# Inner rows of a quantised feed-forward block: turned by DMA in place of TensorE, for tiles 1 to 7

## The chip, the cores and the metric

The kernel runs on one core of one Trainium2 chip. The metric is the device time of one execution in microseconds (us). Each time is the median of several runs. The profile is of one execution of its own.

## What is computed

Two decoder blocks work on x (1024 rows of 512 numbers) and a context of the same size. Each block is an attention over the context and a feed-forward part, both added to x behind a gate. The feed-forward part of the first block is quantised to integers, rows to 8 bits and weights to 4:

```python
def _fake_quant_act(x, n_bits=8):
    scale = max(|x| over the row) / 127
    return clip(round(x / scale), -128, 127) * scale
...
gate = _quant_linear(x, Wg)          # 512 -> 1376
up = _quant_linear(x, Wu)            # 512 -> 1376
h = silu(gate) * up                  # the inner row, 1376 numbers
return _quant_linear(h, Wd)          # 1376 -> 512, the down product
```

The second block is an attention with softmax (queries and keys from the context, values from x) and a small routed low-rank layer on top of a dense one:

```python
R = q @ k ; attention = softmax(R) ; out = attention @ v
y = x @ W_base.T + b_base + sum over experts of alpha * (x @ A.T) @ B.T
```

## The kernel before

x is cut into 8 tiles of 128 rows. A first program (0 to about 555 us) does the whole first attention and prepares the quantised weights. Behind it stands a second program, `last_programs`, which takes the 8 tiles through the quantised feed-forward, the second attention and the routed layer. Several tiles are in flight at once. The order of the work is written out by hand, one list of calls for each of the five engines, and each call waits on semaphores, so an engine never passes a call whose input is late. SyncE (SP) has such a list for its DMAs too.

One tile t goes this way (the names are those of the calls):

- `gate_mm(t, n)`, `up_mm(t, n)` on TensorE for the three column groups n of 512, 512 and 352; `scale_gate`, `scale_up` on VectorE; `tanh_half` on ScalarE; `product` on GpSimd; `make_h(t, n)` on VectorE. The row h is complete after n = 2.
- `h_scales(t)` on VectorE takes the row's largest number; `h_shifted(t)` on ScalarE (L2754) scales h and adds a magic number, so that the low 16 bits of each float are a 2-byte float near 1536 that holds the integer.
- `h_transpose_a(t)` (8 blocks, L1739) and `h_transpose_b(t)` (3 blocks, L1746) on TensorE turn these low halves by a product with an identity, into PSUM banks 4 and 5, which are also those of `gate_mm` and `up_mm`.
- `hT_copy_a(t)` (L2759, 1024 columns) and `hT_copy_b(t)` (L2764, L2765) on ScalarE take off 1536 and write the integers as bf16 into `hqT`.
- `down(t)` (L1754) on TensorE, 11 matmuls of `hqT` with `W.T_d` into bank 4; `output(t)` on VectorE (L2307, tile `f_y`), `add(t)` on GpSimd, and then the statistics, `normalise(t)` and `v_item(t)` of the second attention.

The second attention of tile t has 8 pieces n: `logits(t, n)` on TensorE (L1778, L1779) into bank 0 or 6, `row_max` on VectorE (L2334), `exps` on ScalarE (L2798, tile `b_e`), `reciprocal` for two pieces at a time on VectorE (L2339), `weigh` on GpSimd (L3146), `weights_T` on TensorE (L1788) into bank 3, `copy_T` on ScalarE (L2807, tile `b_eT`), and `attend_pair`. Three limits set how far TensorE may go ahead: `logits` number m waits until `exps` number m-2 has read the bank; `weights_T` number m waits for `weigh` m and for `copy_T` m-1, since bank 3 is one; and `row_max` stands in VectorE's list in a fixed place beside `output`.

SP issues `load_ctx` (context of later tiles), `duplicate` (L1638, five DMAs that lay out queries and keys) and `store`.

Of the kernel before, what the change touches and what calls it, by code (L numbers as in the profile page):

```python
# [7 lines left out]
ACT = mybir.ActivationFunctionType  # L8
# [6 lines left out]
P = 128  # L15
B, S, D = 16, 64, 512
NT = B * S // P
DC = D // P
# [1493 lines left out]
def late_buffers(cx, K):  # L1512
# [75 lines left out]
    M.low_w = take("l1_low", [P, DC, P + E_ACT])  # L1588
    M.bT = M.e[0]
# [51 lines left out]
def last_programs(cx, K, M, W, W1, L0, ctx_dram, out_dram):  # L1641
# [3 lines left out]
    if True:  # L1645
# [27 lines left out]
        s_hTa, s_hTa_sb = sem("s_f_hTa"), sem("s_f_hTa_sb")  # L1673
        s_hTb, s_hTb_sb = sem("s_f_hTb"), sem("s_f_hTb_sb")
# [34 lines left out]
        def tensor(pe, first):  # L1709
# [26 lines left out]
            def h_transpose_a(t):  # L1736
                pe.wait_ge(s_hq, t + 1)
                for c in range(8):
                    mm = pe.transpose(hT_a[:, c, :], low_half(h[t % 2])[:, c * P:(c + 1) * P], K.ident_b[:, :])  # L1739
                mm.then_inc(s_hTa, 1)  # L1740

            def h_transpose_b(t):
                pe.wait_ge(s_hq, t + 1)
                for c in range(8, FT):
                    w = P if c < FT - 1 else FL
                    mm = pe.transpose(hT_b[0:w, c - 8, :], low_half(h[t % 2])[:, c * P:c * P + w], K.ident_b[:, :])  # L1746
                mm.then_inc(s_hTb, 1)

            def down(t):
                pe.wait_ge(s_hTa_sb, t + 1)  # L1750
                pe.wait_ge(s_hTb_sb, t + 1)
# [57 lines left out]
            def x3_T(t):  # L1809
# [3 lines left out]
                if t == NT - 1:  # L1813
                    pe.wait_ge(s_hTb_sb, NT)
# [98 lines left out]
            h_transpose_b(0)  # L1913
            pe.wait_ge(s_gate, 6)
            h_transpose_a(0)
            pe.wait_ge(s_qk_lo[1], 3)
            qk(2, 0)
            pe.wait_ge(s_hTb_sb, 1)
            up_mm(1, 2)
            weights_T(0, 5)  # L1920
            pe.wait_ge(s_hTa_sb, 1)
# [25 lines left out]
            pe.wait_ge(s_gate, 8)  # L1947
            h_transpose_a(1)
            logits(1, 6)
            pe.wait_ge(s_up, 8)  # L1950
            h_transpose_b(1)
# [3 lines left out]
            pe.wait_ge(s_hTa_sb, 2)  # L1955
            gate_mm(2, 2)
            logits(1, 7)
            pe.wait_ge(s_hTb_sb, 2)
# [26 lines left out]
            pe.wait_ge(s_up, 10)  # L1985
            h_transpose_b(2)
# [5 lines left out]
            pe.wait_ge(s_gate, 11)  # L1992
            h_transpose_a(2)
            logits(2, 5)
            pe.wait_ge(s_hTb_sb, 3)
            up_mm(3, 1)
            weights_T(2, 1)
            pe.wait_ge(s_hTa_sb, 3)
            down(2)
            logits(2, 6)  # L2000
            weights_T(2, 2)
            logits(2, 7)
            pe.wait_ge(s_out, 3)
            gate_mm(3, 2)
            weights_T(2, 3)
            pe.wait_ge(s_up, 11)
            up_mm(3, 2)
# [18 lines left out]
            pe.wait_ge(s_gate, 12)  # L2026
            h_transpose_a(3)
            pe.wait_ge(s_up, 12)
            h_transpose_b(3)
# [6 lines left out]
            pe.wait_ge(s_hTa_sb, 4)  # L2036
# [1456 lines left out]
```

## Time and profile before

| | us |
|---|---|
| median of 3 runs (770.85 to 773.05) | 772.27 |
| the profiled execution | 772.25 |
| its span, first to last instruction | 770.4 |
| PE (TensorE) busy | 747.7, 97% |
| DVE (VectorE) busy | 593.2, 77% |
| ACT (ScalarE) busy | 489.8, 64% |
| POOL (GpSimd) busy | 500.3, 65% |

Busy shares are of the whole span. PE's are modelled from the starts of its instructions, so that a short wait can hide in them. The time of an execution is 1.85 us more than its span.

### The profile page before, as it was taken

The numbers are of one execution on the slowest core, as the hardware profiler recorded it, in microseconds if no ns is written. First come the engines' busy times: TensorE is split into PE (matmuls) and PEld (weight loads), VectorE is DVE, ScalarE is ACT, GpSimd is POOL, SyncE is SP. The second block draws the span as 40 slices with busy tenths as digits, with TensorE's granted clock in tenths as the row PEclk, the third lists the DMA queues.
The fourth block names the chain that finished last, engine by engine and source line by source line (L and its number), as shares of the span: only waits on it lengthen the run. The fifth ranks groups of instructions, "written<-read, shape, count | busy, mean of one in ns | idle before, by whom it ended". The sixth has DMA issues, their size and how long they took to land.

```text
span 770.4 us, 13672 instructions
## 1 busy us (share of the span) xinstructions
PE 747.7 (97%) x4829; PEld 594.3 (77%) x4829; DVE 593.2 (77%) x1138; ACT 489.8 (64%) x1082; POOL 500.3 (65%) x431
## 2 busy tenths in 40 slices
PE   8998899999999999999999999997999999999997
PEld 7876688888888888888878888775656777787776
DVE  5888888867788776677866666777899997898863
ACT  5756666665567545665555555354589898888772
POOL 2678676656657865567884557645377877787762
PEclk9999999999999999999999999998999999999999
DMA  9310454433453133241224201265254333122101
GB/s 339 115 68 28 130 113 98 119 83 102 115 133 91 51 99 93 71 130 52 69 57 107 68 1 44 27 257 163 68 152 104 90 91 89 39 64 59 49 18 40
DMA packets 74640, 71.03 MB, mean 92 GB/s; under 512 B 48412, under 2 KB 49660, under 8 KB 74188
## 3 DMA queue, kind: packets, MB, share of 16 engines
q1 hardware_dynamic: 74284, 69.82, 32.2%
q8 instruction: 39, 0.64, 0.3%
q10 hardware_dynamic: 288, 0.33, 0.2%
q14 instruction: 29, 0.24, 0.1%
HBM read 49.04 MB, written 6.34 MB: 72 GB/s over the span
## 4 chain that ended last, share of the span: by engine, by line
PE 83%; DVE 7%; ACT 4%; POOL 3%; issue 1%; DMA 1%; SPq 0%; DVEq 0%
PE bank L81 11%; PE bank L83 10%; PE bank L82 10%; PE bank L591 7%; PE bank L596 6%; PE bank L592 6%; PE bank L1802 4%; PE bank L573 4%; PE bank L675 4%; PE bank L1788 3%; PE bank L1754 2%; PE bank L1725 2%; PE bank L1733 2%; PE bank L1778 2%; PE bank L1779 2%
## 5 line engine op out<-in xcount | busy, mean ns | idle before, releaser
L1346 POOL TENSOR_TENSOR rope_swap<-rope_swap,trig 128x512 f32<-128x512 f32 x80 | 105.2, 1315 | 135.0 <-ACT rope_swap L761 134.7
L1055 DVE SCALAR_TENSOR_TENSOR x_res<-bank,gate,x_res 128x512 f32<-128x512 f32 x128 | 95.5, 746 | 54.1 <-PE bank L596 53.8
L888 ACT CAST oT_hi<-bank 128x512 fp32r<-128x512 f32 x64 | 34.4, 590 | 126.3 <-PE bank L675 126.3
L591 PE MATMUL bank<-wo_hi,oT_hi 128*128 128x512 f32 x256 | 102.4, 400 | 7.2 <-DVE x_res L1055 6.7
L81 PE MATMUL bank<-xnT_hi,wq_hi 128*128 128x512 f32 x252 | 101.5, 403 | 0.0
L592 PE MATMUL bank<-wo_lo,oT_hi 128*128 128x512 f32 x256 | 101.4, 396 | 0.0
L83 PE MATMUL bank<-xnT_hi,wq_lo 128*128 128x512 f32 x252 | 100.0, 397 | 0.0
L82 PE MATMUL bank<-xnT_lo,wq_hi 128*128 128x512 f32 x252 | 99.5, 395 | 0.0
L1352 POOL TENSOR_TENSOR q_rope<-rope_cos,rope_swap 128x512 f32<-128x512 f32 x64 | 82.9, 1295 | 5.0
L596 PE MATMUL bank<-wo_hi,oT_lo 128*128 128x512 f32 x256 | 80.7, 397 | 4.3 <-DVE oT_lo L1211 4.3
L3146 POOL TENSOR_TENSOR b_e<-b_e,b_inv 128x512 f32<-128x512 f32 x64 | 68.3, 1081 | 18.9 <-DVE b_inv L2339 18.4
L1012 DVE TENSOR_TENSOR rope_cos<-bank,trig 128x512 f32<-128x512 f32 x80 | 53.9, 674 | 30.1 <-PE bank L83 26.2
L768 ACT COPY row_other<-row_max 32x16 f32<-32x16 f32 x256 | 51.6, 202 | 23.8 <-DVE row_max L1026 15.5
L760 ACT COPY rope_swap<-bank 64x512 f32<-64x512 f32 x80 | 46.7, 584 | 29.1 <-DVE rope_cos L1012 26.0
L591 PEld LDWEIGHTS bank<-wo_hi,oT_hi 128*128 128x128 f32 x256 | 48.9, 191 | 20.1 <-DVE x_res L1055 9.1
L596 PEld LDWEIGHTS bank<-wo_hi,oT_lo 128*128 128x128 f32 x256 | 48.8, 191 | 15.6 <-DVE oT_lo L1211 5.2
L81 PEld LDWEIGHTS bank<-xnT_hi,wq_hi 128*128 128x128 f32 x252 | 47.3, 188 | 13.0 <-issue 0.3
L592 PEld LDWEIGHTS bank<-wo_lo,oT_hi 128*128 128x128 f32 x256 | 48.9, 191 | 10.5
L1359 POOL TENSOR_TENSOR prob<-prob,row_inv 128x512 f32<-128x512 f32 x32 | 33.6, 1049 | 35.1 <-DVE row_inv L1046 35.1
L83 PEld LDWEIGHTS bank<-xnT_hi,wq_lo 128*128 128x128 f32 x252 | 47.3, 188 | 11.1
L82 PEld LDWEIGHTS bank<-xnT_lo,wq_hi 128*128 128x128 f32 x252 | 47.3, 188 | 10.7
L761 ACT COPY rope_swap<-bank 64x512 f32<-64x512 f32 x80 | 46.3, 578 | 0.9
(277 smaller groups left out, 1955.4 us busy)
## 6 DMA issues: line engine op xcount, KB each, us to landing
wq_raw<-in_wq_tiles SPq DMA_DIRECT2D x16, 512.0 KB, 3.7
wo_raw<-in_L_xattn_wo SPq DMA_DIRECT2D x16, 512.0 KB, 4.1
xn<-in_L_ffn_Wd SPq DMA_DIRECT2D x16, 256.0 KB, 2.9
b_ctx<-in_ctx SPq DMA_DIRECT2D x32, 128.0 KB, 2.6
b_k_twice<-b_qk_hi SPq DMA_DIRECT2D x32, 128.0 KB, 2.4
w_T_dram<-w_out SPq DMA_DIRECT2D x28, 128.0 KB, 3.0
w_T<-w_T_dram SPq DMA_DIRECT2D x2, 1376.0 KB, 9.6
xn<-in_L_ffn_Wg SPq DMA_DIRECT2D x10, 256.0 KB, 3.9
```

What stands on the lines that cost most here:

```text
L81: pe.matmul(out, a_hi, b_hi, start=first, stop=False)
L82: pe.matmul(out, a_hi, b_lo, start=False, stop=False)
L83: return pe.matmul(out, a_lo, b_hi, start=False, stop=last)
L591: pe.matmul(out, oT_hi[:, tl, h], wo_hi[jp][:, h, :], start=(h == 0), stop=False)
L592: pe.matmul(out, oT_hi[:, tl, h], wo_lo[jp][:, h, :], start=False, stop=False)
L596: mm = pe.matmul(out, oT_lo[:, tl, h], wo_hi[jp][:, h, :], start=False, stop=(h == 1))
L768: act.copy(row_other[other, U % 2, :], row_max[mine, U % 2, :]).then_inc(s_swap, 1)
L1012: dve.tensor_tensor(out=rope_cos[:, rp, :].rearrange("p (b s) -> p b s", s=S), in0=proj[stream % NPROJ][:, :].rearrange("p (b s) -> p b s" ...
L1055: dve.scalar_tensor_tensor(out=K.x[:, t, :], in0=wo_ps[t % 2][:, :], scalar=K.gate[:, 0:1], in1=K.x[:, t, :], op0=ALU.mult, op1=ALU.add).t ...
L1346: pool.tensor_tensor(out=sw, in0=sw, in1=sin_b, op=ALU.mult).then_inc(s_rope, 1)
L1352: pool.tensor_tensor(out=dst, in0=rope_cos[:, rp, :].rearrange("p (b s) -> p b s", s=S), in1=sw, op=ALU.add).then_inc(s_rope, 1)
L3146: pool.tensor_tensor(out=e[m % 4][:, :], in0=e[m % 4][:, :], in1=inv_total[:, n:n + 1].to_broadcast([P, D]), op=ALU.mult).then_inc(s_w, 1)
```

## The change

For tiles 1 to 7 the turning leaves TensorE. `h_shifted` adds the plain magic number, three calls `h_int(t, n)` on ScalarE take it off and write the integers as bf16 into three new buffers `M.hq`, and SP turns each of them by a DMA transpose straight into `hqT` (`turn_h(t)`). Tile 0 keeps its way. The new buffers lie behind `b_ctx_split` in free memory. The waits of `down`, `make_h` and `x3_T` follow.

```diff
-            def h_transpose_a(t):
-                pe.wait_ge(s_hq, t + 1)
...
             def down(t):
-                pe.wait_ge(s_hTa_sb, t + 1)
-                pe.wait_ge(s_hTb_sb, t + 1)
+                if t == 0:
+                    pe.wait_ge(s_hT_sb, 2)
+                else:
+                    pe.wait_ge(s_hT, 16 * NFG * t)
...
+            def h_int(t, n):
+                lo, w = FGROUPS[n]
+                act.wait_ge(s_hq, t + 1)
+                if t > 1:
+                    act.wait_ge(s_hT, 16 * NFG * (t - 1))
+                if t == 1 and w % P:
+                    act.copy(M.hq[n][:, w:], h[t % 2][:, 0:P - FL])
+                act.activation(M.hq[n][:, 0:w], h[t % 2][:, lo:lo + w], ACT.Copy, bias=-MAGIC).then_inc(s_h_int, 1)
...
+            def turn_h(t):
+                sp.wait_ge(s_down, t)
+                for n, (lo, w) in enumerate(FGROUPS):
+                    c, k = lo // P, -(-w // P)
+                    sp.wait_ge(s_h_int, NFG * (t - 1) + n + 1)
+                    sp.dma_start_transpose(hqT[:, c:c + k, :], M.hq[n][:, 0:k * P]).then_inc(s_hT, 16)
```

The lists are rewritten around it. On TensorE `down(t)` also moves back, past these calls:

| tile | `down(t)` now stands behind |
|---|---|
| 1 | the same calls as before |
| 2 | `logits(2, 6)`, `weights_T(2, 2)`, `logits(2, 7)`, `weights_T(2, 3)` as well |
| 3 | `weights_T(3, 2)`, `up_mm(4, 0)` as well |
| 4 | `weights_T(4, 4)` as well |
| 5 | `weights_T(5, 4)` as well |
| 6 | the same calls as before |
| 7 | `logits(7, 7)`, `weights_T(7, 3)` as well |

In tile 2 `up_mm(3, 2)` also changes places with `gate_mm(3, 2)`. VectorE's and GpSimd's lists stay as they are.

TensorE in tile 2 before, from `logits(2, 5)` (bank 6) to `weights_T(2, 3)`, the row of `b_e3`; L1754 is `down(2)`, L1733 and L1725 are `up_mm` and `gate_mm`:

```order
L1778 MATMUL bank6<-b_k_twice01_159,b_q_stack01_151 128x512
L1779 MATMUL bank6<-b_k_lo01_155,b_q_stack01_151 128x512
L1733 MATMUL bank5<-w_T1_50,f_xqT_147 128x512 x4
L1788 MATMUL bank3<-ident,b_e1_163 128x128 x4
L1754 MATMUL bank4<-wd_T_51,f_hqT_99 128x512 x11
L1778 MATMUL bank0<-b_k_twice00_158,b_q_stack00_150 128x512
L1779 MATMUL bank0<-b_k_lo00_154,b_q_stack00_150 128x512
L1788 MATMUL bank3<-ident,b_e2_164 128x128 x4
L1778 MATMUL bank6<-b_k_twice01_159,b_q_stack01_151 128x512
L1779 MATMUL bank6<-b_k_lo01_155,b_q_stack01_151 128x512
L1725 MATMUL bank4<-w_T0_49,f_xqT_147 128x352 x4
L1788 MATMUL bank3<-ident,b_e3_165 128x128 x4
```

TensorE in the same place now; L1761 is `down(2)`, L1785 and L1786 are `logits`, L1795 is `weights_T`, L1738 is `up_mm`:

```order
L1785 MATMUL bank6<-b_k_twice01_159,b_q_stack01_151 128x512
L1786 MATMUL bank6<-b_k_lo01_155,b_q_stack01_151 128x512
L1738 MATMUL bank5<-w_T1_50,f_xqT_147 128x512 x4
L1795 MATMUL bank3<-ident,b_e1_163 128x128 x4
L1785 MATMUL bank0<-b_k_twice00_158,b_q_stack00_150 128x512
L1786 MATMUL bank0<-b_k_lo00_154,b_q_stack00_150 128x512
L1795 MATMUL bank3<-ident,b_e2_164 128x128 x4
L1785 MATMUL bank6<-b_k_twice01_159,b_q_stack01_151 128x512
L1786 MATMUL bank6<-b_k_lo01_155,b_q_stack01_151 128x512
L1795 MATMUL bank3<-ident,b_e3_165 128x128 x4
L1761 MATMUL bank4<-wd_T_51,f_hqT_99 128x512 x11
```

`down(2)` stood before `logits(2, 6)` and stands now behind `weights_T(2, 3)`.

ScalarE in tile 2 before, behind `h_shifted(2)`, from `exps(2, 3)` to `exps(2, 4)`; L2764, L2765 and L2759 are the copies of the turned row, L2807 is `copy_T`:

```order
L2798 ACTIVATE b_e3_165,b_total_92<-bank6,b_neg_max_91 128x512
L2764 ACTIVATE f_hqT_99<-bank5 128x256
L2765 ACTIVATE f_hqT_99<-bank5 96x128
L2776 CAST b_ctx_split0_148<-b_ctx0_71 128x512
L2807 COPY b_eT0_166<-bank3 128x4x128
L2759 ACTIVATE f_hqT_99<-bank4 128x1024
L2771 ACTIVATE b_qk_hi0_69<-bank2,l1_bias_54 128x512
L2750 ACTIVATE f_tanh0_107<-f_gate0_138 128x512
L2807 COPY b_eT1_167<-bank3 128x4x128
L2798 ACTIVATE b_e0_162,b_total_92<-bank0,b_neg_max_91 128x512
```

ScalarE in the same place now; L2744 is `h_int`, L2764 is the split of the context, L2795 is `copy_T`, L2786 is `exps`:

```order
L2786 ACTIVATE b_e3_165,b_total_92<-bank6,b_neg_max_91 128x512
L2744 ACTIVATE f_hq_wide_171<-f_h0_67 128x512
L2764 CAST b_ctx_split0_148<-b_ctx0_71 128x512
L2744 ACTIVATE f_hq_wide_171<-f_h0_67 128x512
L2795 COPY b_eT0_166<-bank3 128x4x128
L2744 ACTIVATE f_hq_rest_172<-f_h0_67 128x352
L2759 ACTIVATE b_qk_hi0_69<-bank2,l1_bias_54 128x512
L2730 ACTIVATE f_tanh0_107<-f_gate0_138 128x512
L2795 COPY b_eT1_167<-bank3 128x4x128
L2786 ACTIVATE b_e0_162,b_total_92<-bank0,b_neg_max_91 128x512
```

The copies of the turned row are gone, and the three of the row that is not yet turned stand apart from each other; what is between and behind them keeps its order.

SP before tile 5's place, from the loads and duplicates of tile 6 (`ctx1` is the context of tile 7):

```order
L1638 DMA b_q_stack00_150<-b_qk_hi0_69 64x512
L1638 DMA b_q_stack00_150<-b_qk_lo0_110 64x512
L1638 DMA b_k_twice00_158<-b_qk_hi0_69 64x512 x2
L1638 DMA b_k_lo00_154<-b_qk_lo0_110 64x512
L1628 DMA b_ctx1_72<-in_ctx_4096 64x512 x2
L1638 DMA b_q_stack01_151<-b_qk_hi1_70 64x512
L1638 DMA b_q_stack01_151<-b_qk_lo1_111 64x512
L1638 DMA b_k_twice01_159<-b_qk_hi1_70 64x512 x2
L1638 DMA b_k_lo01_155<-b_qk_lo1_111 64x512
```

SP in the same place now:

```order
L1633 DMA b_ctx1_72<-in_ctx_4096 64x512 x2
L3357 DMA_TRANSPOSE f_hqT_99<-f_hq_wide_171 128x4x128 x2
L3357 DMA_TRANSPOSE f_hqT_99<-f_hq_rest_172 128x3x128
L1643 DMA b_q_stack01_151<-b_qk_hi1_70 64x512
L1643 DMA b_q_stack01_151<-b_qk_lo1_111 64x512
L1643 DMA b_k_twice01_159<-b_qk_hi1_70 64x512 x2
L1643 DMA b_k_lo01_155<-b_qk_lo1_111 64x512
L3361 DMA out_0<-b_result0_112 128x512
L1643 DMA b_q_stack10_152<-b_qk_hi0_69 64x512
```

`turn_h(5)` stands between the load and the duplicates of `duplicate(6, 1)`.

## Rows read from the trace of the kernel before

**Rows 1.** The page's chain by engine, then busy time by stretch: PE, PEld, DVE, ACT, POOL, clock.
```profile
PE 83%; DVE 7%; ACT 4%; POOL 3%; issue 1%; DMA 1%; SPq 0%; DVEq 0%
...
600.00:640.00 40.00, 40.00 (x346) 31.10 (x345) 34.81 (x81) 36.15 (x74) 31.03 (x30) 1.00 0.38 94
...
720.00:770.00 50.00, 45.11 (x359) 35.92 (x357) 31.66 (x84) 29.37 (x68) 25.48 (x25) 0.98 0.13 41
```

**Rows 2.** Waits of PE from 560 to 770 us: the longest in total.
```profile
PE bank L1746 <- ACT f_h L2754: 0.8, 1, 0.8
```

**Rows 3.** Timeline, tile 1 (start, us, engine, line, op, tiles, count): PE, then ACT.
```profile
593.91 0.62 PE L1739 MATMUL bank<-ident_b,f_h 128*128 128x128 bf16 x8
...
594.34 0.48 PE L1778 MATMUL bank<-b_k_twice,b_q_stack 128*128 128x512 f32 x1
...
600.59 2.55 PE L1754 MATMUL bank<-wd_T,f_hqT 128*128 128x512 bf16 x11
...
591.62 1.44 ACT L2754 ACTIVATE f_h<-f_h,f_h_inv 128x1376 f32<-128x1376 f32 x1
```

**Rows 4.** The instructions of one line on ACT: inner row copied from PSUM; tanh.
```profile
L2759 ACT ACTIVATE f_hqT<-bank x8: 1023/1023/1030, 579.1 to 741.2; 128x1024 bf16<-128x1024 f16 x8
...
L2750 ACT ACTIVATE f_tanh<-f_gate x24: 483/626/684, 556.5 to 729.9; 128x512 f32<-128x512 f32 x16, 128x352 f32<-128x352 f32 x8
```

**Rows 5.** The instructions of line 368, the DMA transposes of the weights.
```profile
L368 SPq DMA_TRANSPOSE w_out<-w_quant x34: 1180/1272/2226, 78.1 to 435.2; - x34
...
DMA to landing us min/median/max: 2.3/2.9/6.1
```

**Rows 6.** Timeline of PE, tile 2: down product, then weights_T(2, 3) and weights_T(2, 4).
```profile
619.13 2.54 PE L1754 MATMUL bank<-wd_T,f_hqT 128*128 128x512 bf16 x11
...
623.50 0.60 PE L1788 MATMUL bank<-ident,b_e 128*128 128x128 f32 x4
...
625.00 0.60 PE L1788 MATMUL bank<-ident,b_e 128*128 128x128 f32 x4
```

**Rows 7.** Timeline around tile 2: ACT, DVE, POOL.
```profile
620.94 0.69 ACT L2798 ACTIVATE b_e<-bank,b_neg_max 128x512 f32<-128x512 f32 x1 [0.17 <-DVE b_neg_max L2334]
...
621.62 0.80 ACT L2737 ACTIVATE f_xn<-x_res,f_shift,f_rstd 128x512 f32<-128x512 f32 x1
...
622.62 0.59 ACT L2807 COPY b_eT<-bank 128x512 f32<-128x512 f32 x1 [0.20 <-PE bank L1788]
...
620.23 0.68 DVE L2334 TENSOR_REDUCE b_neg_max<-bank 128x1 f32<-128x512 f32 x1
...
621.71 0.75 DVE L2307 SCALAR_TENSOR_TENSOR f_y<-bank,f_h_gate,wd_row 128x512 f32<-128x512 f32 x1
...
623.83 2.04 POOL L3146 TENSOR_TENSOR b_e<-b_e,b_inv 128x512 f32<-128x512 f32 x2
```

**Rows 8.** Timeline, tiles 3, 4, 5, 7: each down product and what its successor waited for.
```profile
642.15 2.54 PE L1754 MATMUL bank<-wd_T,f_hqT 128*128 128x512 bf16 x11
...
641.99 2.04 POOL L3146 TENSOR_TENSOR b_e<-b_e,b_inv 128x512 f32<-128x512 f32 x2 [2.64 <-DVE b_inv L2339]
...
670.61 2.54 PE L1754 MATMUL bank<-wd_T,f_hqT 128*128 128x512 bf16 x11
...
670.36 2.34 POOL L3146 TENSOR_TENSOR b_e<-b_e,b_inv 128x512 f32<-128x512 f32 x2 [0.87 <-DVE b_inv L2339]
...
696.21 2.55 PE L1754 MATMUL bank<-wd_T,f_hqT 128*128 128x512 bf16 x11
...
697.22 0.60 ACT L2807 COPY b_eT<-bank 128x512 f32<-128x512 f32 x1
...
742.46 2.55 PE L1754 MATMUL bank<-wd_T,f_hqT 128*128 128x512 bf16 x11
...
743.29 0.71 ACT L2798 ACTIVATE b_e<-bank,b_neg_max 128x512 f32<-128x512 f32 x1
```

**Rows 9.** Busy time and clock of a stretch after a long wait of PE.
```profile
535.00:540.00 5.00, 4.07 (x10) 2.67 (x10) 3.61 (x8) 4.78 (x12) 3.22 (x3) 0.50 0.01 2
```

## What was predicted

> **What bounds the kernel now.** I read the chain that ended last first, and the busy time by stretch beside it: TensorE holds 83% of the chain, and between 600 and 640 us it is busy for 40.00 of 40.00 us at the full granted clock [rows 1]. Only the last 50 us show it idle for some 5. Then the waits: the longest that TensorE has between 560 and 770 us is 0.8 us, and that is in tile 0, which the change leaves alone [rows 2]. So in the part that the change touches TensorE's list sets the end, any TensorE work taken out of it counts in full, and any new wait of TensorE counts in full as well. What the second program is full of, though, is short loops: logits, row maximum, exponential, reciprocal, weighing, turning, all passing through TensorE again. Whether there are new waits is therefore read from the timelines of the other engines: for each call behind which `down` now stands, when was its input there?
>
> All sums are made against the profiled execution, 772.25 us (a span of 770.4 and 1.85 around it). The median of the runs is 772.27, so nothing has to be carried over.
>
> **What is removed.** Eight of the eleven block transposes of a tile take 594.34 - 593.91 = 0.43 us of TensorE's list, from the first of them to the instruction behind them [rows 3]; eleven take 11/8 of that, 0.59. Seven tiles give 4.1 us. If nothing else changed the kernel would take 768.1.
>
> **What ScalarE gets.** Before, a copy of 1024 columns of 1.02 us, and two small ones. Now three copies of 512, 512 and 352 columns; the nearest row is the tanh of the same widths, 0.63 and 0.48 [rows 4]. That is 2 x 0.63 + 0.48 = 1.73 in place of 1.02 plus two small ones of together some 0.65, equal within 0.1 us for a tile. They can't be free, since they stand before other calls, but they also can't cost more than a few tenths: the wait of ScalarE for TensorE's transposes goes. I set it at zero beyond the times that I walk through below. The extra copy of 32 columns in tile 1 is one short instruction, 0 to 0.2 us.
>
> **The turn by DMA.** No row shows this turn, but 34 turns of the same width do: 1.27 us for SP to issue one, 2.9 us (2.3 to 6.1) from issue to landing [rows 5]. Three in a row take 2 x 1.3 + 2.9 = 5.5 us from the first copy's end, or 2.9 from the last copy's end if the copies come slower than SP issues. In tile 1 `h_shifted` starts at 591.62 and takes 1.44, one exponential and the first copy follow, so that the first turn goes out at 594.2 and the last lands at 599.7. `down(1)` started at 600.59 [rows 3], and comes at 600.0 without its 0.59: there is 0.3 us to spare. In tiles 2 to 7 the same walk lands each turn 0.9 to 2.3 us before the place where `down` now stands. So I cost the DMA at nothing, with 0 to 3 us as its bounds (3 is the longest landing of the row against the median). SP's own list is pushed back by 3.8 us of issues per tile. Behind `turn_h(5)` waits `duplicate(6, 1)`, for `logits(6, 1)`; it would land near 700.5, just when TensorE gets there, and the other duplicates have more time. Zero, at most 0.5.
>
> **Tile 1.** 0.59 goes. But TensorE soon stands before `v_item(1)`, which waits for a chain on VectorE and GpSimd that moves up by 0.2 only. I take -0.2 (bounds -0.6 and, with a late turn, +3).
>
> **Tile 2, the large term.** `down(2)` started at 619.13 [rows 6], in the time in which ScalarE had not yet done `exps(2, 4)` and `exps(2, 5)`. Now four attention calls stand before it, and I ask what the last two wait for. `logits(2, 7)` needs `exps(2, 5)`, which started at 620.94 behind the row maximum at 620.23 [rows 7]; that row maximum follows `up_mm(3, 1)`, which is 0.59 earlier, and so `exps(2, 5)` runs from 620.3 to 621.0. `weights_T(2, 3)` needs bank 3 free, that is `copy_T(2, 2)`, and that one stands on ScalarE behind the normalisation of 0.80 us (621.62 before, 621.0 now) and takes 0.59 [rows 7]: it ends at 622.3. TensorE has 1.4 us of work to do between 618.5 and there, and waits 2.4 us. With 0.44 for `weights_T(2, 3)` itself, `down(2)` starts at 622.8 in place of 619.13: 3.65 us later, where it was a filler before.
>
> Then VectorE. Its list is unchanged, and in it `output(2)` stands before `reciprocal(2, 2)` and `row_max(2, 6)`. It ran at 621.71 [rows 7], 2.58 behind the start of the down product, and runs at 625.4 now. All that stands behind it moves by 3.65: GpSimd's `weigh(2, 4)`, the first of the two from 623.83 [rows 7], ended at 624.87, and TensorE took `weights_T(2, 4)` at 625.00 [rows 6]. So 0.1 of slack, and `weights_T(2, 4)` starts at 628.5: +3.5 us, the saved transposes already in it. Bounds: +2.5, if ScalarE gets to `copy_T(2, 2)` a microsecond earlier than I walk it, and +4.2.
>
> **Tile 3.** `weights_T(3, 2)` needs `weigh(3, 2)`, the first of two from 641.99 [rows 8], at its end at 643.0. `down(3)` began at 642.15 and covered that; now nothing does. With the chain 0.59 earlier, TensorE waits 0.9 at 641.6, does `up_mm(4, 0)`, and starts `down(3)` at 643.8 in place of 642.15. The row maxima behind `output(3)` move by 1.6 and have some 0.7 to spare. I take +0.7 (0 to +1.3).
>
> **Tile 4.** `weights_T(4, 4)` needs `weigh(4, 4)`, the first of two from 670.36 [rows 8], ended at about 671.6, and this chain hangs on VectorE and isn't earlier. `down(4)` began at 670.61. Now 671.6 + 0.44 = 672.0 is its start. The pair ends 1.0 later than before: +1.0 (0 to +1.5).
>
> **Tile 5.** `weights_T(5, 4)` needs `copy_T(5, 3)`, at 697.22 for 0.60 [rows 8]; 0.6 earlier at best. `down(5)` began at 696.21 and starts at 697.65 now; the pair ends 1.1 later (+0.3 to +1.5).
>
> **Tile 6.** Nothing moves, 0.59 goes: -0.6.
>
> **Tile 7.** `logits(7, 7)` needs `exps(7, 5)`, at 743.29 [rows 8], earlier by the 0.9 of the large copy that leaves: it ends at 743.2. Then `weights_T(7, 3)`, and `down(7)` at 744.15 in place of 742.46. The last `v_item(7)` hangs on it through `output(7)`, and comes 1.3 later: +1.3 (+0.5 to +2).
>
> **The sum.** -0.2 + 3.5 + 0.7 + 1.0 + 1.1 - 0.6 + 1.3 = +6.8. That is 779.0 us, slower by 0.9%. The delays add up because TensorE has no idle time between the tiles in which to make them good, and the loops of each tile start from TensorE again.
>
> **The rivals.**
>
> (A) *The time of the transposes is gained.* Then the calls now before `down` have their inputs in time, and the wait for the turned row is what would have cost. This would be so if the other engines ran ahead once TensorE lets go of banks 4 and 5. 772.25 - 4.1 = 768.1. Against it: the rows of tile 2 name two calls that can't start, and one of them only needs ScalarE's own order. Chance 14%. The Trainium skill ("DMA: Bandwidth & Descriptors", Rules for kernel authors) has it that a DMA is to be issued early and waited for late, with compute between; by that rule the change is right and 768.1 is its time. The trace agrees only on the DMA's part: the 2.9 us would be covered. The rule doesn't ask whether the compute put between is ready, and here it isn't.
>
> (B) *Only tile 2 loses.* In tiles 3 to 7 the late engines catch up during tile 2's wait, the weighing is in time, and each of the five gains its 0.59: 3.5 - 0.2 - 3.0 = +0.3, 772.6. For it: VectorE is busy for 34.81 of 40 us [rows 1], so it has a little room. Against it: tiles 4 and 5 wait for things that start from TensorE's own calls of the same tile. Chance 14%.
>
> (C) *The turns are late as well.* With landings near 6.1 us in place of 2.9 [rows 5] and spare times of 0.3 in tile 1 and about 0.9 in tile 5, TensorE waits 2.9 and 2.3 more: 784.2. Chance 8%.
>
> (D) *TensorE's clock falls after the wait in tile 2.* The profile before has one such place: after a wait of some 3.4 us the clock that was granted between 535 and 540 us was 0.50, the lower of the two levels (1.2 in place of 2.4 GHz) [rows 9]. A stretch of 10 us at that level has 5 us less work in it: 784. My wait of 2.4 us is broken by matmuls, so I give it 6%. The Trainium skill ("TensorE: Matmul & The Clock Gate", Why this matters for your kernels) tells to keep TensorE free of idle gaps between bursts of matmuls, since the clock goes back; by that the moved `down` would be doubly wrong and the time 784, and the row of 535 us agrees that it happens.
>
> **The numbers.** The forecast, 776 to 782, has the remaining 58%. I call it slower if above 774.6, faster if below 769.9, since 0.3% is about what a measurement of this kernel can tell from no change. Slower: forecast, (C) and (D), 0.72. Same: (B), 0.14. Faster: (A), 0.14. The range reaches from 771.0, which takes (B) and the low ends of the terms, to 785.0, which takes (C) and (D); (A) and a little on either side stay outside.
>
> **What would show it.** In the profile after, TensorE waits where none was: some 2.4 us before `logits(2, 6)`, `logits(2, 7)` and `weights_T(2, 3)`, released by ScalarE's `b_e` and `b_eT`; then about 1 us before `weights_T(2, 4)`, released by GpSimd; 0.7 to 1.5 before `weights_T(3, 2)`, `weights_T(4, 4)`, `weights_T(5, 4)` and `logits(7, 7)`. From the start of `down(1)` to that of `down(2)` it is 18.5 us before and should be some 22.8. No wait of `down` for a DMA is expected. The forecast is wrong if `down(2)` follows `weights_T(2, 1)` closely, if `weights_T(2, 4)` doesn't wait, or if TensorE waits for DMA at all.

## The result and the profile after

The changed kernel takes 779.58 us (median of 6 runs, 778.31 to 780.75) where the kernel before takes 771.51 (6 runs). The ratio is 1.0103, with a 95% interval of 1.0091 to 1.0114. The forecast was 779.0, slower by 0.9%. The profiled execution took 780.75 us with a span of 778.9. The ratio isn't that of the two medians: in the experiments the two differ by up to 1.0 us (e12), mostly by 0.1 to 0.6, so it's said where a number comes from one of them.

The chain of the page by engine, after. TensorE's share has fallen from 83% to 76% [rows 1]; VectorE, GpSimd, ScalarE and "issue" have each taken a piece of it.

```profile
PE 76%; DVE 9%; POOL 6%; ACT 5%; issue 3%; DMA 1%; SPq 1%; DVEq 0%; ACTq 0%; POOLq 0%
```

Busy time by stretch, after (stretch, its length, PE, PEld, DVE, ACT, POOL, clock, DMA share, GB/s):

```profile
600.00:640.00 40.00, 36.56 (x279) 26.69 (x282) 32.39 (x79) 32.40 (x68) 29.89 (x29) 1.00 0.39 97
640.00:680.00 40.00, 37.66 (x279) 26.54 (x278) 31.56 (x72) 34.27 (x73) 28.69 (x26) 1.00 0.35 82
680.00:720.00 40.00, 38.31 (x316) 29.78 (x318) 34.24 (x74) 30.96 (x67) 31.01 (x29) 1.00 0.27 67
720.00:780.00 60.00, 52.42 (x381) 40.70 (x382) 36.43 (x97) 34.97 (x79) 30.37 (x30) 0.99 0.17 46
```

Between 600 and 640 us TensorE was full [rows 1] and is now idle for 3.44 us. The granted clock is 1.00 in the first three stretches and 0.99 in the last, so it stays at its upper level for nearly all of the time.

The waits of PE from 560 to 780 us, after (line waited for, its releaser: us in total, times, longest). Before, the longest of this stretch was the one of tile 0 that is still here, 0.8 us [rows 2].

```profile
PE bank L1785 <- ACT b_e L2786: 3.8, 3, 1.6
PE bank L1795 <- ACT b_eT L2795: 3.7, 8, 1.5
PE bank L1795 <- POOL b_e L3141: 1.2, 2, 0.8
PE bank L1751 <- ACT f_h L2735: 0.8, 1, 0.8
PE bank L1785 <- DMA b_k_lo<-b_qk_lo: 0.6, 1, 0.6
```

`down` (L1761) isn't in this list. It never waits for its turned row, and the calls put in front of it do the waiting: `logits` (L1785) for an exponential, `weights_T` (L1795) for a copy or for GpSimd.

TensorE in tile 2, after. A bracket gives the idle time before the row and what ended it.

```profile
619.47 0.60 PE L1795 MATMUL bank<-ident,b_e 128*128 128x128 f32 x4
621.68 0.50 PE L1785 MATMUL bank<-b_k_twice,b_q_stack 128*128 128x512 f32 x1 [1.62 <-ACT b_e L2786]
...
622.61 0.48 PE L1785 MATMUL bank<-b_k_twice,b_q_stack 128*128 128x512 f32 x1
...
623.62 0.63 PE L1795 MATMUL bank<-ident,b_e 128*128 128x128 f32 x4 [0.30 <-ACT b_eT L2795]
624.09 2.54 PE L1761 MATMUL bank<-wd_T,f_hqT 128*128 128x512 bf16 x11
...
627.48 0.77 PE L1730 MATMUL bank<-w_T,f_xqT 128*128 128x352 bf16 x4 [0.25 <-DVE f_y L2287]
629.03 0.47 PE L1785 MATMUL bank<-b_k_twice,b_q_stack 128*128 128x512 f32 x1 [0.79 <-ACT b_e L2786]
...
629.88 0.66 PE L1795 MATMUL bank<-ident,b_e 128*128 128x128 f32 x4
```

The rows are `weights_T(2, 1)`, `logits(2, 6)`, `logits(2, 7)`, `weights_T(2, 3)`, `down(2)`, `gate_mm(3, 2)`, `logits(3, 0)` and `weights_T(2, 4)`. In the kernel before `down(2)` began at 619.13 [rows 6] and covered the time in which ScalarE wasn't ready.

`weights_T(2, 4)` has no bracket, but it waits too. It starts 0.54 us behind the start of the matmul before it (629.34 in the trace), where before the change this was 0.23 (624.77 to 625.00). Its input is the first of the two weighings in this row of GpSimd, done after 1.03 us, at 629.8:

```profile
628.78 2.04 POOL L3141 TENSOR_TENSOR b_e<-b_e,b_inv 128x512 f32<-128x512 f32 x2
```

Two traces must be laid on each other with care. The second program (the one with these tiles) starts 1.36 us later in the profiled execution after, since in the first program, whose code is the same, the two executions differ. So I count each tile by the start of `v_item(t)` less that of `v_item(0)`. Before, the eight of them start at 589.23, 609.12, 630.30, 656.97, 678.88, 705.05, 732.87 and 750.82 us. The lag of a kernel is by how much more it needs to get from `v_item(0)` to `v_item(t)`:

| kernel | start | v 1 | v 2 | v 3 | v 4 | v 5 | v 6 | v 7 | ratio [95%] |
|---|---|---|---|---|---|---|---|---|---|
| after | 1.36 | 0.04 | 3.59 | 4.28 | 5.48 | 6.52 | 6.49 | 8.26 | 1.0103 [1.0091, 1.0114] |
| e1_down_back | 0.29 | 0.04 | 1.80 | 2.49 | 3.01 | 3.89 | 3.69 | 4.67 | 1.0058 [1.0044, 1.0071] |
| e2_before_down_late | 1.66 | 0.03 | 4.39 | 5.68 | 6.88 | 8.59 | 8.58 | 10.72 | 1.0155 [1.0140, 1.0171] |
| e3_down2_back | 0.23 | 0.04 | 1.81 | 2.48 | 3.68 | 4.70 | 4.54 | 7.97 | 1.0093 [1.0078, 1.0107] |
| e4_short_turn2 | -0.07 | -0.01 | -0.48 | -0.93 | -0.99 | -1.44 | -1.80 | -1.98 | 0.9982 [0.9973, 0.9992] |
| e5_vector_first | -0.13 | 0.03 | 3.39 | 4.15 | 5.34 | 6.38 | 5.98 | 7.75 | 1.0096 [1.0083, 1.0109] |
| e6_int_together | 0.17 | 0.99 | 2.23 | 2.36 | 3.00 | 2.33 | 1.82 | 2.36 | 1.0027 [1.0017, 1.0036] |
| e7_two_turns | -0.65 | 0.04 | 1.96 | 1.69 | 2.21 | 3.05 | 2.56 | 3.00 | 1.0045 [1.0031, 1.0058] |
| e12_ready_again | 1.13 | 0.03 | 2.18 | 1.58 | 2.09 | 3.00 | 2.49 | 3.92 | 1.0046 [1.0031, 1.0062] |
| e9_together_two | 0.65 | 0.02 | 0.57 | -0.02 | 0.61 | -0.07 | -0.61 | -0.64 | 0.9982 [0.9973, 0.9991] |
| e10_together_one | -1.08 | 0.03 | 0.76 | 0.19 | 0.81 | 0.08 | -0.43 | -0.45 | 0.9985 [0.9975, 0.9994] |
| e11_one_down_late | -1.01 | 0.03 | 3.55 | 4.29 | 6.21 | 7.25 | 6.74 | 8.73 | 1.0101 [1.0083, 1.0119] |

### The profile page after: what moved, and what is told of

Its sections match the earlier page's. It is cut to its first block, busy times and chain, and to the rows that moved or that the text cites. A ratio compares the mean times of both kernels' runs of the same rounds, so it can differ in the third digit from the quotient of the medians.

```text
span 778.9 us, 13515 instructions
## 1 busy us (share of the span) xinstructions
PE 745.7 (96%) x4736; PEld 590.4 (76%) x4752; DVE 591.4 (76%) x1138; ACT 489.4 (63%) x1083; POOL 499.3 (64%) x431
## 4 chain that ended last, share of the span: by engine, by line
PE 76%; DVE 9%; POOL 6%; ACT 5%; issue 3%; DMA 1%; SPq 1%; DVEq 0%; ACTq 0%; POOLq 0%
PE bank L81 11%; PE bank L83 10%; PE bank L82 10%; PE bank L591 6%; PE bank L596 6%; PE bank L592 6%; PE bank L573 4%; PE bank L675 4%; PE bank L1809 3%; PE bank L1795 3%; PE bank L1761 2%; PE bank L1730 2%; PE bank L1738 1%; PE bank L1785 1%; POOL rope_swap L1346 1%
## 5 line engine op out<-in xcount | busy, mean ns | idle before, releaser
L760 ACT COPY rope_swap<-bank 64x512 f32<-64x512 f32 x80 | 46.7, 584 | 31.1 <-DVE rope_cos L1012 28.0
L2786 ACT ACTIVATE b_e<-bank,b_neg_max 128x512 f32<-128x512 f32 x64 | 44.1, 690 | 12.0 <-DVE b_neg_max L2314 11.9
```

## The experiments

The change has two halves: the transposes leave TensorE for a DMA, and `down` moves back. The first two kernels take one half each.

**e1_down_back.** The changed kernel with its down products in the old places:

```diff
+            pe.wait_ge(s_gate, 11)
+            down(2)
             logits(2, 6)
             weights_T(2, 2)
             logits(2, 7)
-            weights_T(2, 3)
-            pe.wait_ge(s_gate, 11)
-            down(2)
...
```

> The changed kernel, with the down products of tiles 2, 3, 4, 5 and 7 back in their old places in TensorE's list; the turn by DMA and the three integer copies stay. Theory (the order costs, since down stands behind calls whose inputs are late): most of the loss goes. What is left is that down(2) now waits for its turn: in the changed kernel the last turn of tile 2 was issued at 619.8 and landed 2.4 us later, some 1.7 us behind the old start of down(2) when both are counted from the start of the second program. Tiles 3, 5 and 7 wait 0.1 to 0.5, tile 4 gains 0.5. Sum about +2 us on the kernel before: ratio 1.001 to 1.005. Rival (the DMA turns and SP's longer list cost): still 1.008 to 1.012.

It gave 776.1 us, 1.0058 [1.0044, 1.0071]. So 4.6 us (by the medians) of the loss of 8.07 stay when the places are the old ones. The ratio lies between the ranges of the two theories, which end at 1.005 and begin at 1.008. Its waits of PE:

```profile
PE bank L1761 <- DMA f_hqT<-f_hq_rest: 5.5, 4, 2.2
PE bank L1795 <- ACT b_eT L2795: 1.9, 6, 0.6
```

Now `down` does wait for the turn, 5.5 us in four places: 2.25 us in tile 2, where 1.7 was expected, and 1.16, 0.83 and 1.29 in tiles 3, 5 and 7, where 0.1 to 0.5 was. In the old places the turn is late; in the new ones it is covered, by calls that wait themselves.

**e2_before_down_late.** The kernel before with its transposes and the late places of `down`, the mirror of e1.

> The kernel before, with its transposes on TensorE and its copies, but with the down products of tiles 2, 3, 4, 5 and 7 in the later places of the changed kernel. No DMA turn. Theory (order): all of the loss is there and the 0.59 us of transposes for a tile on top: +8 to +11 us, ratio 1.010 to 1.014, with TensorE waiting before logits(2, 6), logits(2, 7) and weights_T(2, 3). Rival (DMA): within 0.3% of the kernel before, ratio 0.997 to 1.003.

It gave 783.22 us, 1.0155 [1.0140, 1.0171], a little above what was expected. The late places alone cost 11.7 us (by the medians). The same three waits appear as in the changed kernel (L1778 is `logits` there and L1788 `weights_T`):

```profile
PE bank L1778 <- ACT b_e L2798: 3.8, 3, 1.5
PE bank L1788 <- ACT b_eT L2807: 2.8, 4, 1.6
PE bank L1788 <- POOL b_e L3146: 1.8, 2, 1.0
```

**e3_down2_back.** The changed kernel with `down(2)` alone (and with it `gate_mm(3, 2)` and `up_mm(3, 2)`) in its old place.

> The changed kernel, with the down product of tile 2 alone back in its old place. Theory: tile 2 is half of the loss. Its 3.6 us become the 1.7 that the turn by DMA is late: 1.9 us less than the changed kernel, +6 us on the kernel before, ratio 1.007 to 1.009, and the first item behind it, weights_T(2, 4), doesn't wait for GpSimd. Rival (the delays don't add up, and a wait that goes in tile 2 comes back in tile 3): 1.010 as the changed kernel.

It gave 778.52 us, 1.0093 [1.0078, 1.0107]. The lag at `v_item(2)` falls from 3.59 to 1.81, and 2.24 us of wait for the turn stand in place of the other waits. But tile 7 takes 3.43 (7.97 less 4.54) where it takes 1.77 in the changed kernel. There the clock fell. Around `down(7)` of e3, first the stretches, then TensorE:

```profile
745.00:750.00 5.00, 3.41 (x18) 2.32 (x17) 3.68 (x11) 3.63 (x9) 4.39 (x5) 0.89 0.23 46
750.00:755.00 5.00, 4.78 (x18) 2.65 (x18) 1.20 (x2) 1.27 (x3) 1.17 (x2) 0.77 0.00 0
```

```profile
748.55 0.51 PE L1785 MATMUL bank<-b_k_twice,b_q_stack 128*128 128x512 f32 x1 [1.40 <-ACT b_e L2786]
...
749.28 1.05 PE L1795 MATMUL bank<-ident,b_e 128*128 128x128 f32 x4
750.56 3.19 PE L1761 MATMUL bank<-wd_T,f_hqT 128*128 128x512 bf16 x10 [0.22 <-issue]
```

Behind a wait of 1.40 us `weights_T(7, 3)` takes 1.05 us instead of 0.60, and ten matmuls of `down(7)` take 3.19 where the same ten take 2.32 in the changed kernel. A granted clock of 0.89 and 0.77, each over 5 us, stands for 3 to 4 us in all at the lower of the two levels (1.2 in place of 2.4 GHz), since (0.11 + 0.23) x 5 us lost at half speed are 3.4 us. The changed kernel has the same wait, 1.41 us, in the same place, and its clock stayed at 1.00. In e3 itself the longer wait of 2.24 us before `down(2)` also left it at 1.00.

**e4_short_turn2.** The kernel before without eight of the eleven transposes of tiles 1 to 7 (the copies read three blocks several times, so the down product is computed from other numbers). It prices TensorE's time alone.

> The kernel before, in tiles 1 to 7 with 3 of the 11 block transposes on TensorE and 8 left out; the copies on ScalarE stay as wide as they were, and read the one block several times. It leaves out the turning of 8 of 11 blocks, and so computes the down product of those tiles from other numbers. It measures what the removed TensorE time is worth. If every microsecond of TensorE counts (0.43 us for each of 7 tiles): -3.0 us, ratio 0.996. If the waits of v_item(1) and v_item(6) for the statistics swallow what tiles 1 and 6 save, as the trace of the changed kernel suggests: -2 us, ratio 0.997 to 0.998. Rival (other engines set the pace all along): 1.000.

It gave 770.27 us, 0.9982 [0.9973, 0.9992]: 1.4 us (by the ratio) for the 3.0 taken away, and 1.98 by the lag at `v_item(7)`. That is the second of its three theories. Tiles 1 and 4 give nothing or next to it (0.01 and 0.06 us), tile 7 gives 0.18 and tile 6 gives 0.36. In tile 1 the time comes back before `v_item(1)`, which waits for the normalised row:

```profile
609.04 1.13 PE L1765 MATMUL bank<-l_v,b_xn 128*128 128x128 f32 x8 [0.39 <-ACT b_xn L2781]
```

A stretch in which PE was busy for 40.00 of 40.00 us [rows 1] is not one in which TensorE alone sets the pace:

```profile
600.00:640.00 40.00, 39.35 (x326) 30.46 (x330) 34.83 (x81) 36.03 (x76) 30.95 (x30) 1.00 0.37 93
```

**e5_vector_first.** The prediction has the delay in tile 2 go on through VectorE's list, where `output(2)` stands before the next row maxima. The changed kernel with that undone:

```diff
-            output(2)
             reciprocal(2, 2)
             row_max(2, 6)
             row_max(2, 7)
+            output(2)
...
-            add(2)
             weigh(2, 4)
             weigh(2, 5)
+            add(2)
```

> The changed kernel with one more move, in tile 2 alone: on VectorE reciprocal(2, 2), row_max(2, 6) and row_max(2, 7) stand ahead of output(2), on GpSimd weigh(2, 4) and weigh(2, 5) ahead of add(2). TensorE's order stays that of the change. In the trace of the changed kernel VectorE sat idle for 4.70 us before output(2), ScalarE for 4.63 us before exps(2, 6) behind it, GpSimd for 4.52 us before add(2). Theory (the late down product costs through VectorE's order, in which output(2) stands before the row maxima): TensorE's waits of 0.79 us before logits(3, 0) and of 0.8 us before weights_T(2, 4) go, v_item(2) comes 1.2 to 1.6 us earlier, and the ratio to the kernel before goes from 1.0103 to about 1.0085. Rival (what costs is only that down(2) itself stands behind calls that are not ready, so that VectorE's order is a symptom): the ratio stays at 1.010.

It gave 779.85 us, 1.0096 [1.0083, 1.0109], not to be told from the changed kernel. The wait of 0.79 us before `logits(3, 0)` is gone, as the theory has it, and so is the one before `weights_T(2, 4)` (0.3 us in the trace, where the expectation has 0.8). But `v_item(2)` comes only 0.20 us earlier, since it waits itself now:

```profile
633.56 1.13 PE L1772 MATMUL bank<-l_v,b_xn 128*128 128x128 f32 x8 [0.52 <-ACT b_xn L2769]
```

Its input goes over `output(2)`, `add(2)` and `statistics(2)`, the last two in these rows of GpSimd and VectorE:

```profile
625.99 1.27 POOL L3131 TENSOR_TENSOR x_res<-f_y,x_res 128x512 f32<-128x512 f32 x1 [2.31 <-DVE f_y L2287]
...
627.29 0.69 DVE L2292 BATCH_NORM_STATS2 b_stats<-x_res 128x6 f32<-128x512 f32 x1 [1.39 <-POOL x_res L3131]
```

Both engines stand idle for it. The calls set ahead were done long before, and `statistics(2)` starts 4.71 us behind `down(2)` (at 622.58), as in the changed kernel (4.77). `v_item(2)` starts 10.98 us behind `down(2)`, where it was 11.16. So the rival holds: the normalised row that `v_item(2)` needs hangs on `down(2)` itself, and what costs is its place, not the order of VectorE's list.

The next experiments, up to e10, look into the 4.6 us that e1 keeps.

**e6_int_together.** e1 with the three copies of a tile directly behind `h_shifted`:

```diff
             h_shifted(2)
+            h_int(2, 0)
+            h_int(2, 1)
+            h_int(2, 2)
             exps(2, 3)
-            h_int(2, 0)
             split_hi(5, 0)
...
```

> e1_down_back (down products in their old places, turn by DMA), with the three h_int calls of every tile directly behind h_shifted on ScalarE, where exponentials and copies stood between them. In e1_down_back down waited 5.5 us in four places for the last turn. Theory (the turn is late because ScalarE's copies are spread): the last copy ends 1.5 to 3 us earlier, the turns go out one behind the other at 1.26 us each, the waits of down fall by 0.6 us in tile 2 and by 0.8 to 1.0 in tiles 3, 5 and 7, and the ratio goes from 1.0058 to about 1.003. Rival (ScalarE's time is the scarce thing: the copies of attention that are pushed back by up to 1.8 us hold TensorE in their place): the waits of down shrink, others before weights_T appear, and the ratio stays at 1.005 to 1.007.

It gave 774.13 us, 1.0027 [1.0017, 1.0036], as the theory has it. The waits of `down` fall from 5.5 to 2.7 us. Tile 1 pays for it with 0.99 us, since `exps(1, 4)` now stands behind three copies and `logits(1, 6)` waits 1.51 us for it (the expectation for e9 calls it `logits(1, 7)`, and its 1.17 us for this tile has the later start of the program in it). In the waits it is the third row:

```profile
PE bank L1761 <- DMA f_hqT<-f_hq_rest: 2.7, 3, 1.5
PE bank L1795 <- ACT b_eT L2795: 1.5, 5, 0.5
PE bank L1785 <- ACT b_e L2786: 1.5, 1, 1.5
```

**e7_two_turns.** e1 with two turns for a tile, of 1024 and of 384 columns:

```diff
-                for n, (lo, w) in enumerate(FGROUPS):
-                    c, k = lo // P, -(-w // P)
+                for n, c, k, source in ((1, 0, 2 * DC, M.hq_wide), (2, 2 * DC, FT - 2 * DC, M.hq[2])):
```

> e1_down_back with two turns for each tile in place of three: one of 1024 columns behind the second h_int, one of the last 384. Theory A (the issue of a turn by SP is a fixed 1.26 us): the 1024 columns are issued in about 1.3 us as well, the last turn goes out up to 1 us earlier in tiles 3 and 7 and as before in 2 and 5, ratio 1.004 to 1.0055. Theory B (the issue grows with the columns): it takes about 2.5 us, the last turn goes out 1.2 us later or just as late, the waits of down grow from 5.5 to 7 to 10 us, ratio 1.006 to 1.010.

It gave 774.89 us, 1.0045 [1.0031, 1.0058]. The instructions of the turn's line, first in the changed kernel, then in e7 (duration ns min/median/max):

```profile
L3357 SPq DMA_TRANSPOSE f_hqT<-f_hq_wide x14: 1188/1258/1667, 595.7 to 747.1; - x14
...
DMA to landing us min/median/max: 2.4/2.4/3.1
```

```profile
L3357 SPq DMA_TRANSPOSE f_hqT<-f_hq_wide x7: 1232/1242/2440, 594.7 to 740.9; - x7
...
DMA to landing us min/median/max: 2.4/2.9/3.7
```

The 2.9 is over the turns of both widths. Those of 1024 columns alone, by their source `f_hq_wide`, land later:

```profile
DMA to landing us min/median/max: 3.2/3.3/3.7
```

1024 columns are issued in 1.24 us, as 512 are in 1.26. Up to this width the issue has the same price, and theory A holds. The waits of `down` are 4.1 us in place of 5.5: less in tiles 3 and 7 (0.20 and 0.74), and no less in tiles 2 and 5 (2.38 and 0.81), as it said.

**e8_ready_first and e12_ready_again.** e1 with `logits(2, 6)` and `weights_T(2, 2)` ahead of `down(2)`, `up_mm(4, 0)` ahead of `down(3)` and `logits(7, 7)` ahead of `down(7)`. One execution of e8, the profiled one, took three times as long as all others, so its trace is of no use, and e12 is the same kernel again.

> e1_down_back with calls that have their inputs ahead of a down that waits for its turn: logits(2, 6) and weights_T(2, 2) ahead of down(2), up_mm(4, 0) ahead of down(3), logits(7, 7) ahead of down(7). Theory (down is a filler that has to stand behind what is ready, and not behind what isn't): some 1.2 us of the wait of 2.2 in tile 2, 0.5 of 1.2 in tile 3 and 0.7 of 1.3 in tile 7 are filled, ratio 1.0028 to 1.004 where e1_down_back gave 1.0058. Rival (every call set ahead of down pushes output(t) back and with it VectorE's list, so that the filled time comes back): 1.005 or more.

> The kernel of e8_ready_first once more, for its trace (that of the first was of a broken execution, 2561 us long). Theory (the calls set ahead fill the wait for the turn): down(2) waits about 1.0 us in place of 2.2, down(3) about 0.7 in place of 1.2 and down(7) about 0.6 in place of 1.3. Rival (the filled time comes back behind output(t)): the waits of down fall as said, but v_item(2) and v_item(3) come no earlier than in e1_down_back, with lags of 1.8 and 2.5 us against the kernel before.

They gave 1.0048 [1.0035, 1.0061] and 1.0046 [1.0031, 1.0062], where e1 gave 1.0058; the intervals overlap, so the places are read from the trace of e12. The three places don't go alike. Tile 3 takes 0.60 less than before the change instead of 0.69 more, since `up_mm(4, 0)` was ready. Tile 2 takes 2.15 instead of 1.76 and tile 7 takes 1.43 instead of 0.98, since `logits(2, 6)` and `logits(7, 7)` were not. `down(2)`, `down(3)` and `down(7)` don't wait any more, but these two do:

```profile
621.44 0.50 PE L1785 MATMUL bank<-b_k_twice,b_q_stack 128*128 128x512 f32 x1 [1.62 <-ACT b_e L2786]
...
747.39 0.50 PE L1785 MATMUL bank<-b_k_twice,b_q_stack 128*128 128x512 f32 x1 [1.40 <-ACT b_e L2786]
```

I had taken both for ready. So neither theory was right as a whole: a call that is ready in front of the product gains, one that isn't costs, and which is which has to be read for each.

**e9_together_two and e10_together_one.** The old places, the copies together in tiles 2 to 7, and two turns or one for a tile.

> Down products in the old places, h_int calls together behind h_shifted in tiles 2 to 7 (tile 1 left as in the change, since e6_int_together lost 1.17 us there, with a wait of 1.51 us before logits(1, 7)), and two turns for a tile as in e7_two_turns. Theory (what remained in e1_down_back was the turn's lateness, made of ScalarE's spread copies and SP's 1.26 us for each issue): the waits of down fall to 1 us or less in tile 2 and to about 0 in the others, ratio 0.999 to 1.0015. Rival (the gains of e6_int_together and e7_two_turns overlap, since both take away the same wait, and the copies pushed back on ScalarE cost): ratio 1.002 to 1.003, as e6_int_together gave.

> As e9_together_two, with one turn of all 1408 columns for each tile, behind the third h_int (f_xn changes its place in memory for it, so that the copies lie in a row). SP issues one transfer in place of three. Theory (the issue is a fixed 1.26 us, and the landing barely depends on the columns: 2.4 us for 512 and 2.9 for 1024): the turn lands 2.5 to 3.3 us behind the last copy, down(2) waits 0.3 to 0.8 us and the other down products not at all, ratio 0.997 to 1.000, so faster than the kernel before by up to the 4.1 us of the transposes less what tiles 1 and 2 keep. Rival (the landing grows with the columns): it takes 3.5 to 5 us, ratio above that of e9_together_two.

They gave 770.84 us, 0.9982 [0.9973, 0.9991], and 770.32 us, 0.9985 [0.9975, 0.9994]. Both are faster than the kernel before by 1.2 to 1.4 us (by the ratios), and some 9 us faster than the changed kernel. They can't be told from each other. By the lag at `v_item(7)` only 0.64 and 0.45 us of it are gained in the tiles; the rest is of the size of the 1.15 us that every kernel with the turn by DMA gains at its end (last section). The turn of all 1408 columns is issued in 1.39 us and lands after 3.5, later than the theory's 2.5 to 3.3: the landing does grow with the columns. `down(2)` waits 0.97 us for it and 0.79 in e9, so what the one issue fewer saves the landing takes back. The waits of `down` in e9 and in e10, and the turn of e10:

```profile
PE bank L1762 <- DMA f_hqT<-f_hq_rest: 0.8, 1, 0.8
```

```profile
PE bank L1761 <- DMA f_hqT<-f_hq_all: 1.0, 1, 1.0
```

```profile
L3355 SPq DMA_TRANSPOSE f_hqT<-f_hq_all x6: 1319/1387/1416, 615.1 to 737.1; - x6
...
DMA to landing us min/median/max: 3.5/3.5/3.6
```

**e11_one_down_late.** e10 with the late places of the change.

> e10_together_one with the five down products in the late places of the change. Theory (the late places cost by themselves, about as much as in e2_before_down_late, where they cost 11.7 us with the transposes kept, and a quicker turn gives nothing back, since the changed kernel's down products never waited for it): +8.5 to +11.5 us on e10_together_one, ratio 1.0095 to 1.0135, near the 1.0103 of the changed kernel. Rival (half of the loss of the changed kernel was the spread of ScalarE's copies): the quicker turn and the copies together make the late places cheaper, ratio 1.003 to 1.006.

It gave 779.6 us, 1.0101 [1.0083, 1.0119], like the changed kernel: 9.3 us by the medians for the places alone (a lag of 8.73 in place of -0.45 gives 9.2). A quicker turn helps nothing where nobody waits for the turn.

## Why the prediction was right, point by point

**The mechanism** is the one foretold: the calls now ahead of `down` aren't ready, and the product can no longer fill their wait. e2 and e11 show it twice, without the DMA and with the best DMA, at 11.7 and 9.3 us.

**The terms**, each as the growth of the lag from one `v_item` to the next:

| tile | predicted | after |
|---|---|---|
| 1 | -0.2 | +0.04 |
| 2 | +3.5 | +3.55 |
| 3 | +0.7 | +0.69 |
| 4 | +1.0 | +1.20 |
| 5 | +1.1 | +1.04 |
| 6 | -0.6 | -0.03 |
| 7 | +1.3 | +1.77 |
| sum | +6.8 | +8.26 |

Tiles 2 to 5 are within 0.2 us. From `down(1)` to `down(2)` it takes 22.1 us (22.3 with the first matmul of `down(1)`, whose record is missing in the trace); 22.8 was named, for 18.5 before. The 2.4 us of waits before `down(2)` came as 1.62 and 0.30, and `down(2)` was 3.6 us late.

**Tile 2, what comes behind.** The walk came out almost to the number. `weights_T(2, 4)` was to start at 628.5 and starts at 629.88, which is 628.52 less the later start of 1.36, and it starts 0.06 us behind the end of the weighing on GpSimd, as foretold. Only the wait is split: `logits(3, 0)`, ahead of it, takes 0.79 us, for an exponential behind the late row maximum, and some 0.3 is left for GpSimd. What the prediction had too simple is that the delay passes on through the order of VectorE's list. That is true of these two waits but not of the time: e5 takes both away and gets 0.2 us back, since `v_item(2)` also hangs on `down(2)` over `output(2)`, `add(2)` and `statistics(2)`, and that way is as long.

**Tiles 3, 4, 5 and 7.** The four calls wait for what was named (0.48 to 1.52 us, where 0.7 to 1.5 was said):

```profile
647.42 0.65 PE L1795 MATMUL bank<-ident,b_e 128*128 128x128 f32 x4 [0.77 <-POOL b_e L3141]
...
677.41 0.66 PE L1795 MATMUL bank<-ident,b_e 128*128 128x128 f32 x4 [0.48 <-POOL b_e L3141]
...
704.11 0.63 PE L1795 MATMUL bank<-ident,b_e 128*128 128x128 f32 x4 [1.52 <-ACT b_eT L2795]
...
751.63 0.50 PE L1785 MATMUL bank<-b_k_twice,b_q_stack 128*128 128x512 f32 x1 [1.41 <-ACT b_e L2786]
```

Tile 7 lost 0.47 us more than its term. `exps(7, 5)` was to be earlier by the 0.9 us of the large copy that leaves ScalarE. It started at 743.29 before [rows 8] and starts at 750.80 now. Counted from `v_item(6)` (732.87 and 740.72) that is 10.42 and 10.08 us, only 0.34 earlier. It stands behind `copy_T(7, 2)`, for which ScalarE waits 0.64 us for TensorE.

**Tiles 1 and 6**, where only the transposes' 0.59 should have gone, show nothing of it. In tile 6 the term that failed is SP's pushback, set at zero with 0.5 as its bound. `turn_h(6)` now stands before a store and `duplicate(7, 1)`, and `logits(7, 1)` waits for it:

```profile
735.25 0.50 PE L1785 MATMUL bank<-b_k_twice,b_q_stack 128*128 128x512 f32 x1 [0.62 <-DMA b_k_lo<-b_qk_lo]
```

The prediction names as a sign against itself that TensorE waits for a DMA at all. By this row it does, though not for a turned row. Where the wait is shorter tile 6 gains more: it is 0.49, 0.46, 0.25 and 0.17 us in e3, e1, e5 and e7, and tile 6 gains 0.16, 0.20, 0.40 and 0.49. In e6, e12, e9, e10 and e11, where it isn't there, tile 6 gains 0.51 to 0.54, nearly the 0.59 foretold. Two of these (e6, e12) have three issues for a tile, so the number of issues doesn't decide alone. I had looked at `duplicate(6, 1)` and given the others "more time" without walking them.

In tile 1 the term was the chain of `v_item(1)` that moves up by 0.2. It doesn't move: the lag is between -0.01 and 0.04 in every kernel but e6, with and without the DMA turn, and in e4 TensorE gets there earlier and waits 0.39 us. `weights_T(1, 1)` waits 0.24 us for a copy that now stands behind the first `h_int`, but `v_item(1)` would have waited for its row in any case. Tiles 1 and 6 are 0.8 of the 1.46 us that the sum lacks, and tile 7 is most of the rest.

**The transposes** were set at 4.1 us, in full. e4 gives 1.4 to 2.0 us for 3.0, and from e2 to the changed kernel, where all of them go and the turn by DMA comes in, `v_item(7)` comes 2.46 us earlier. A wholly busy TensorE was read as "everything taken out counts". It isn't so here: in e4 TensorE is idle for 0.65 us between 600 and 640 us, in the row shown, where before it was idle for none [rows 1]. Of these 0.39 are the wait of `v_item(1)`; the rest is in pieces too small to be listed. The sum came out well since the terms were walked tile by tile, and (A), which rests on the full 4.1, would have been wrong with the best order as well: e9 and e10 gain 1.2 to 1.4 us, and about half of it in the tiles.

**The turn by DMA.** Right for the changed kernel, no wait of `down` in it, so (C) fell. The landing was 2.4 us (3.1 at most) where 2.9 (6.1 at most) was taken. But e1 shows how near it was: the row lands up to 2.2 us behind the old place. Of the Trainium skill's rule ("DMA: Bandwidth & Descriptors", Rules for kernel authors), issue early and wait late with compute between, e6, e9 and e10 bear out the first half, each issued earlier or less often, and e2 and e11 show the price of the second where the compute isn't ready.

**(B) and (D).** Tiles 4 and 5 lost 1.20 and 1.04, so (B) fell. The changed kernel's clock held. In e3 it did fall behind a wait of 1.40 us, and cost some 1.7 us in tile 7 (3.43 against 1.77). That is the mechanism of (D) in a third of its size. The Trainium skill's advice against idle gaps between bursts of matmuls ("TensorE: Matmul & The Clock Gate", Why this matters for your kernels) points the same way. This case agrees with it in e3 alone: the changed kernel kept its clock through waits of 1.62 and 1.41 us.

**Left over.** The start is 1.36 us later in the one profile and the end 1.15 us nearer to the last `v_item`. With the lag of 8.26 this makes the 8.5 by which the spans differ (778.9 less 770.4). The medians differ by 8.07. That 779.0 came so near was in part luck: the 1.46 us that the sum lacks met the 1.15 us at the end, of which the prediction knew nothing, and a base of 772.25, which is 0.74 above the median of the six runs. From 771.51 the same sum gives 778.3.

## What to carry to other kernels

A call that never waits is a filler: before moving it back, read for each call that is to go in front of it when its input is there, and move only behind the ready ones. When work goes from a full engine to a DMA, count the issues on the queue and how early the source is complete; here the old places of `down` took the loss from 1.0% to 0.6% (e1), copies in a row took it to 0.3% (e6), and one or two issues in place of three, with tile 1's copies left apart, made a gain of 0.2% of it (e9, e10), the 1.15 us at the end included. An engine that is busy all the time is not alone in setting the pace: taking 3.0 us out of it gave 1.4 to 2.

## What was not expected of the hardware

The issue of a DMA transpose within the chip's own buffers took 1.26 us for 512 columns, 1.25 for 384, 1.24 for 1024 and 1.39 for 1408. The landing grew more: medians of 2.5, 2.4, 3.3 and 3.5 us.

The clock fell in e3 for 3 to 4 us behind an idle time of 1.40 us, and didn't in the changed kernel behind 1.41 us. Waits of 2.24 and 2.25 us before `down(2)` in e3 and e1 left it at 1.00 as well. What made the difference is open.

The last store of the result lands sooner in every kernel with the turn by DMA. It is the same instruction, and it starts 16.0 us behind `v_item(7)` before and after. The instructions of its line before, then after (the last of the times is the start of the last store):

```profile
L3359 SPq DMA_DIRECT2D out<-b_result x8: 332/338/584, 631.3 to 766.8; - x8
...
DMA to landing us min/median/max: 2.0/2.0/3.8
```

```profile
L3361 SPq DMA_DIRECT2D out<-b_result x8: 332/345/595, 636.2 to 776.4; - x8
...
DMA to landing us min/median/max: 2.0/2.0/2.5
```

The span ends 3.6 us behind the issue before and 2.5 after; it is 3.6 in e2 and e4 as well, the other kernels without the DMA turn, and 2.5 in the rest. So 1.15 us of what the turn by DMA gains aren't TensorE's at all. No run looked for the cause.
